# Leading halves of the first batch's keys and their 32x32 grams ahead of everything, with a layer norm spread through the order

## The reference

```
G = Kc.T @ Kc + 1e-4 * I ;  W = solve(G, Kc.T @ Vc)
U = eye[:, :8];  twice: U, _ = qr(W @ U)
S = 0.9 * S + U @ (U.T @ W)        # S is carried along the 8 chunks of a batch
out = 0.125 * (Qc @ S)
```

## Time and profile before

| | us |
|---|---|
| median of 3 runs (936.78 to 948.41) | 944.77 |
| the profiled execution | 943.76 |
| its span, first to last instruction | 941.7 |
| PE busy in it | 800.1 |
| DVE busy | 621.3 |
| ACT busy | 494.1 |
| POOL busy | 206.7 |

### The profile page before, as it was taken

How to read it: one execution, slowest core, us unless ns; L and a number is a source line. 1 busy time by engine, 2 the same in 40 slices (tenths; PEclk the granted TensorE clock), 3 DMA queues, 4 the chain that set the end, 5 groups by cost and what they waited for, 6 DMA issues and landing times.

```text
span 941.7 us, 36123 instructions
## 1 busy us (share of the span) xinstructions
PE 800.1 (85%) x15690; PEld 535.7 (57%) x15690; DVE 621.3 (66%) x1312; ACT 494.1 (52%) x1068; POOL 206.7 (22%) x265
## 2 busy tenths in 40 slices
PE   5999999999989999896798678783588789958896
PEld 2555555665555555564566457562466556746775
DVE  4880497299997999917566866888996201355664
ACT  2854444564544555544456455543357446636765
POOL 4550000101001100002101432542003101435554
PEclk9999999999988999998799989987599889979998
DMA  8742313753655655865442374311545543212210
GB/s 317 237 158 77 90 46 101 205 163 96 187 150 160 160 142 140 202 195 139 100 98 95 101 189 148 107 52 52 114 116 139 132 90 92 93 42 75 80 46 29
DMA packets 214348, 116.64 MB, mean 124 GB/s; under 512 B 149232, under 2 KB 200816, under 8 KB 213168
## 3 DMA queue, kind: packets, MB, share of 16 engines
q1 hardware_dynamic: 208720, 93.10, 36.5%
q0 software_dynamic: 5472, 21.24, 6.8%
HBM read 61.22 MB, written 53.08 MB: 121 GB/s over the span
## 4 chain that ended last, share of the span: by engine, by line
PE 71%; issue 9%; ACT 7%; DVE 6%; DMA 4%; POOL 2%; SPq 1%; POOLq 0%; DVEq 0%; ACTq 0%
PE psum L1188 23%; PE psum L1350 6%; PE psum L1210 5%; PE psum L1418 5%; PE psum L1408 5%; PE psum L1301 4%; PE psum L1388 3%; PE psum L1266 3%; PE psum L1253 2%; PE psum L1240 2%; PE psum L1288 2%; PE psum L1381 2%; PE psum L1324 2%; ACT ht L918 2%; PE psum L1374 1%
## 5 line engine op out<-in xcount | busy, mean ns | idle before, releaser
L1188 PE MATMUL psum<-wkv,xhat 128*128 128x512 f32 x512 | 245.0, 623 | 4.3 <-ACT xhat L783 4.3
L1049 DVE SCALAR_TENSOR_TENSOR outer<-sweep_mem,rd 128x992 f32<-128x992 f32 (+30 forms) x248 | 190.2, 767 | 8.7
L1055 DVE TENSOR_TENSOR sweep_mem<-sweep_mem,outer 128x992 f32<-128x992 f32 (+30 forms) x248 | 176.1, 710 | 8.5
L1188 PEld LDWEIGHTS psum<-wkv,xhat 128*128 128x128 f32 x512 | 95.4, 196 | 108.4 <-issue 102.9
L791 ACT COPY kv<-psum 128x512 f32<-128x512 f32 x128 | 75.0, 586 | 126.4 <-PE psum L1188 126.2
L918 ACT ACTIVATE ht<-psum,b1c,alpha 128x128 f32<-128x128 f32 x256 | 96.5, 461 | 42.4 <-PE psum L1408 42.4
L713 POOL TENSOR_TENSOR hsplit<-ht,hsplit 128x512 f16<-128x512 f32 x64 | 77.1, 1206 | 159.1 <-ACT hsplit L923 159.0
L1418 PE MATMUL psum<-s2t,hsplit 128*128 128x256 f16 x512 | 69.2, 293 | 5.4 <-POOL hsplit L713 2.7
L1408 PEld LDWEIGHTS psum<-y3t,s1t 128*128 128x128 f16 x1024 | 58.6, 99 | 13.0 <-issue 12.3
L1418 PEld LDWEIGHTS psum<-s2t,hsplit 128*128 128x128 f16 x512 | 53.1, 105 | 19.6 <-issue 6.6
L1408 PE MATMUL psum<-y3t,s1t 128*128 128x128 f16 x1024 | 64.0, 222 | 0.0
(11 more groups left out here) (128 smaller groups left out, 1237.4 us busy)
## 6 DMA issues: line engine op xcount, KB each, us to landing
gc_d<-gc SPq DMA_DIRECT2D x32, 512.0 KB, 3.1
schur_mem<-gc_d SPq DMA_DIRECT2D x32, 384.0 KB, 4.6
f_d<-fac SPq DMA_DIRECT2D x16, 512.0 KB, 3.7
fl<-f_d SPq DMA_DIRECT2D x32, 256.0 KB, 2.7
sv_d<-sv SPq DMA_DIRECT2D x16, 384.0 KB, 2.8
lead_d<-sweep_mem POOLq DMA_DIRECT2D x4, 1024.0 KB, 4.2
schur_mem<-lead_d SPq DMA_DIRECT2D x32, 128.0 KB, 4.3
r_d<-pt SPq DMA_DIRECT2D x16, 256.0 KB, 2.4
```

Source lines behind the costliest of these rows:

```text
L1049: V.scalar_tensor_tensor(out=tile, in0=a[:, t, t + 1:HALF].unsqueeze(2).broadcast_to([P, m, HALF]), scalar=rd[:, t:t + 1], in1=a[:, t, t + ...
L1055: V.tensor_tensor(rest, rest, tile, ALU.subtract).then_inc(swept, 1)
L1188: ins = mm(dst[:], xnt[:, c, t], wkv[:, n, t, BANK * half:BANK * (half + 1)], start=t == 0, stop=t == KT - 1)
```

## The change

1. The layer norm becomes steps LN of ORDER, with 17 groups of 1, 1 and 15 x 2 chunks. `advance_dve` puts one in while DVE's model time is within 4 us of PE's; once a sweep is staged and due, only if fewer than 4 chunks are ahead of the last T.
2. x now lies in pt, the residual in state, and the sweeps have a buffer of their own (work). POOL's wait for the residual stores goes. In its place ACT's evacuation of the first two SP steps waits for all 17 groups (pt is written there), and the first two state updates wait for the residual stores.
3. For the 8 chunks of batch 0 (EARLY = 8) the list begins with T, KL, LG of each chunk: KL projects the leading 32 columns of each head's keys, ACT copies them to keys, LG forms 16 grams of 32x32 from them (both operands 128 rows x 32 columns), ACT copies these to gl0 (in kv), SP stores them to lead_in_d. Then for each of these chunks KC (ACT places the kept leading keys in kv), KT (PE projects the trailing halves), VA, VB, G. The first sweep is staged after the eighth LG. KC of chunk 0 waits for the stores of all eight, as gl0 lies in kv.
4. gc_d no longer has the leading blocks and lies by partition (one piece of 3072 bytes for a chunk and partition). For chunks 8 to 31 ACT copies the leading block of G to gl separately and SP stores it to lead_in_d with two more DMAs.
5. The plan: it starts at 0 and not with fixed offsets; two small steps in a row cost 1.4 times; main stays ahead of tail and lead to its end (MIX_FROM 32); NB of batch 0, 1, 2, 3 is not put before 5, 6, 7, 8 sweeps are done in the plan. The new steps get weights (KL, KT 1.72 and LG .55 on PE; KC, KT, KL .65 and LG .35 on ACT, G 1.35 for 1.1).
6. fac, fl, nb and ht share the memory of keys.

The diff, cut to its core:

```diff
...
-GROUPS = (1, 3) + (4,) * 7
+GROUPS = (1, 1) + (2,) * 15
...
-PE_START, DVE_START = 10.0, 75.0
-MIX_FROM = 22
+EARLY = 8
+LN_WEIGHT = 1.75
+MIX_FROM = 32
+ALONE = 1.4
+TURNS_AFTER = (5, 6, 7, 8)
...
-    now = dict(pe=PE_START, act=PE_START, dve=DVE_START, pool=DVE_START)
+    now = dict(pe=0.0, act=0.0, dve=5.0, pool=5.0)
+    norms = list(range(len(GROUPS)))
+    latest = [""]
     def advance_dve():
+            while norms and now["dve"] <= now["pe"] + 4.0:
+                g = norms[0]
+                behind = FIRST[g] < sum(1 for c in range(NCH) if ("T", c) in where) + 4
+                if staged and staged[0][1] <= now["dve"] + 1.0 and not behind:
+                    break
+                norms.pop(0)
+                order.append(("LN", g))
+                now["dve"] = max(now["dve"], now["pe"] - 2.0) + LN_WEIGHT * GROUPS[g] + .6
+                for c in range(FIRST[g], FIRST[g] + GROUPS[g]):
+                    at["LN", c] = now["dve"]
...
     def follows(step, c):
-        return dict(KA=[("T", c)], KB=[("T", c)], VA=[("T", c)], VB=[("T", c)], G=[("VB", c)], SP=[("LC", c)], SX=[("SP", c)],
+        return dict(T=[("LN", c)], KL=[("T", c)], LG=[("KL", c)], KT=[("T", c)], KA=[("T", c)], KB=[("T", c)], VA=[("T", c)], VB=[("T", c)], G=[("VB", c)], SP=[("LC", c)], SX=[("SP", c)],
...
-            now["pe"] = can_start(step, c) + PE_WEIGHT[step]
+            now["pe"] = can_start(step, c) + PE_WEIGHT[step] * (ALONE if step in SMALL and latest[0] in SMALL else 1)
+            latest[0] = step
...
-        elif step == "G" and c % CPB == CPB - 1:
+        elif step == "LG" and c % CPB == CPB - 1:
+            open_at[0, c // CPB] = at["LG", c] + .5
+        elif step == "G" and c % CPB == CPB - 1 and c >= EARLY:
...
-    main = [("T", 0)]
+    main = [] if EARLY else [("T", 0)]
-        for step in ("KA", "KB", "VA", "VB", "T", "G"):
-            if step != "T" or c + 1 < NCH:
+        if c < EARLY and c % CPB == 0:
+            main += [("T", c), ("KL", c)]
+            for n in range(c + 1, c + CPB):
+                main += [("T", n), ("KL", n), ("LG", n - 1)]
+            main.append(("LG", c + CPB - 1))
+        for step in ("KC", "KT", "VA", "VB", "T", "G") if c < EARLY else ("KA", "KB", "VA", "VB", "T", "G"):
+            if step != "T" or EARLY <= c + 1 < NCH:
...
-    last = "T"
+        if turn in able and turn[0][0] == "NB" and sum(("swept", w, b) in at for w in range(2) for b in range(BATCH)
+                                                                         ) < TURNS_AFTER[TURNS[turn[0][1]] // CPB]:
+            able.remove(turn)
-        stream = large[0] if last in SMALL and large else able[0]
-        last = stream[0][0]
+        stream = large[0] if latest[0] in SMALL and large else able[0]
...
-    gc_d = scratch("gc_d", [NCH, PAIRS, P, P])
+    gc_d = scratch("gc_d", [P, NCH, PAIRS, 3 * HALF])
+    lead_in_d = scratch("lead_in_d", [NCH, HEADS, HALF, HALF])
...
-        sweep_mem = sb("sweep_mem", [P, 4 * 4 * DM])
-        xg = sweep_mem[:, 0:8 * DM].rearrange("p (a k d) -> p a k d", a=2, k=4)
-        lng = sweep_mem[:, 8 * DM:16 * DM].rearrange("p (a k d) -> p a k d", a=2, k=4)
-        work = sweep_mem[:].rearrange("p (a i n) -> p a i n", a=2, i=HALF)
+        work = sb("work", [P, 2, HALF, HD])
-        gc = sb("gc", [P, 2, PAIRS, P])
+        gc = sb("gc", [P, 2, PAIRS, 3 * HALF])
+        gl = sb("gl", [P, 2, PAIRS, HALF])
+        gl0 = kv[:, 0].rearrange("p (c n) -> p c n", n=P)
...
+        xg = pt[:].rearrange("p e c h n -> p (e c h n)").rearrange("p (a k d) -> p a k d", a=2, k=2)
...
-        fac = sb("fac", [P, 2, 2 * DM])
+        late = sb("late", [P, CPB * BANK])
+        keys = late[:].rearrange("p (c n) -> p c n", n=BANK)
+        fac = late[:, 0:4 * DM].rearrange("p (c n) -> p c n", n=2 * DM)
...
-        fl = sb("fl", [P, 3, 2 * DM])
-        nb = sb("nb", [P, 2, DM])
+        fl = late[:, 4 * DM:10 * DM].rearrange("p (a n) -> p a n", n=2 * DM)
+        nb = late[:, 10 * DM:12 * DM].rearrange("p (a n) -> p a n", n=DM)
+        lng = state[:].rearrange("p a (k d) -> p a k d", k=2)
-        ht = sb("ht", [P, FF])
+        ht = late[:, 12 * DM:16 * DM]
...
-                    sp.dma_start(gct[:, n, i], gc_d[c + i].rearrange("h r n -> r h n")[:, :, HALF:P]).then_inc(schur_loaded[n], 16)
+                    sp.dma_start(gct[:, n, i], gc_d[:, c + i]).then_inc(schur_loaded[n], 16)
...
-                src = gc_d[c:c + 2].rearrange("c (s u) r n -> u r c s n", u=2)
+                src = gc_d[:, c:c + 2].rearrange("r c (s u) n -> u r c s n", u=2)
-                        sp.dma_start(cu[rows(2 * a), u], src[u, rows(2 * a), :, :, HD:P]).then_inc(sides_loaded, 16)
+                        sp.dma_start(cu[rows(2 * a), u], src[u, rows(2 * a), :, :, HALF:]).then_inc(sides_loaded, 16)
             def load_factors(r):
...
-                    sp.dma_start(gc_d[c].rearrange("h r n -> r h n"), gc[:, c % 2]).then_inc(gc_stored[c % 2], 16)
+                    sp.dma_start(gc_d[:, c], gc[:, c % 2]).then_inc(gc_stored[c % 2], 16)
+                    if c >= EARLY:
+                        dst = lead_in_d[c].rearrange("(h a) r n -> a r h n", a=2)
+                        for a in range(2):
+                            sp.dma_start(dst[a], gl[rows(2 * a), c % 2]).then_inc(lead_in_stored[c % 2], 16)
+                elif step == "LG":
+                    sp.wait_ge(*is_drained("LG", c))
+                    sp.dma_start(lead_in_d[c].rearrange("(k q) r n -> (q r) k n", q=QUADS), pieces(gl0[:, c % CPB], HALF)
+                                 ).then_inc(lead_in_stored[c % 2], 16)
...
-            for g, size in enumerate(GROUPS):
+            def norm(g):
+                size = GROUPS[g]
...
-                else:
-                    for n in range(2):
-                        pool.wait_ge(res_stored[n], 16 * len(GROUPS[n::2]))
-                eye = sweep_mem[:, HALF * HD * (j % 2) + HALF:HALF * HD * (j % 2 + 1):HD + 1]
+                eye = work[:, j % 2].rearrange("p i n -> p (i n)")[:, HALF::HD + 1]
-                        pool.wait_ge(gc_stored[n], 16 * CPB // 2 * (b + 1))
-                    src = gc_d[CPB * b:CPB * (b + 1), :, :, 0:HALF].rearrange("c h (s r) n -> (c h s) r n", s=2)[:, 0:HALF]
+                        pool.wait_ge(lead_in_stored[n], 16 * CPB // 2 * (b + 1 + max(0, b + 1 - EARLY // CPB)))
+                    src = lead_in_d[CPB * b:CPB * (b + 1)].rearrange("c h r n -> (c h) r n")
...
-                if step == "SLOAD":
+                if step == "LN":
+                    norm(c)
+                elif step == "SLOAD":
...
+            def early_keys(c):
+                act.wait_ge(*is_filled("KL", c))
+                if c >= CPB:
+                    act.wait_ge(keys_placed, c - CPB + 1)
+                    act.wait_ge(*is_filled("LG", c - CPB))
+                nc.scalar.copy(keys[:, c % CPB], place("KL", c)).then_inc(drain("KL", c), 1)
+            def early_gram(c):
+                act.wait_ge(*is_filled("LG", c))
+                if c >= CPB:
+                    act.wait_ge(*is_filled("G", CPB - 1))
+                nc.scalar.copy(gl0[:, c % CPB], place("LG", c)[:, 0:P]).then_inc(drain("LG", c), 1)
+            def by_halves(c):
+                return kv[:, 0].rearrange("p (h u e) -> p h u e", u=2, e=HALF)
+            def place_keys(c):
+                if c % CPB == 0:
+                    for n in range(2):
+                        act.wait_ge(lead_in_stored[n], 16 * (c + CPB) // 2)
+                else:
+                    act.wait_ge(*is_filled("G", c - 1))
+                act.wait_ge(*is_drained("KL", c))
+                nc.scalar.copy(by_halves(c)[:, :, 0], pieces(keys[:, c % CPB], HALF)).then_inc(keys_placed, 1)
+            def late_keys(c):
+                act.wait_ge(*is_filled("KT", c))
+                nc.scalar.copy(by_halves(c)[:, :, 1], pieces(place("KT", c), HALF)).then_inc(drain("KT", c), 1)
             def projected(step, c, n, half):
...
             def gram(c):
-                nc.scalar.copy(gc[:, c % 2].rearrange("p h n -> p (h n)"), place("G", c)).then_inc(drain("G", c), 1)
+                src = pieces(place("G", c), P)
+                if c >= EARLY:
+                    wait(act, lead_in_stored[c % 2], 16 * EARLY // 2 + 32 * ((c - EARLY) // 2))
+                    nc.scalar.copy(gl[:, c % 2], src[:, :, 0:HALF])
+                nc.scalar.copy(gc[:, c % 2], src[:, :, HALF:]).then_inc(drain("G", c), 1)
             def signs(n):
...
             def leading_inverse(e):
+                if e < 2:
+                    act.wait_ge(res_ready, len(GROUPS))
...
-            for g, size in enumerate(GROUPS):
+            def norm(g):
+                size = GROUPS[g]
...
-                    dg = sweep_mem[:, HALF * HD * (j % 2):HALF * HD * (j % 2 + 1):HD + 1]
+                    dg = a.rearrange("p i n -> p (i n)")[:, ::HD + 1]
...
+                else:
+                    for n in range(2):
```

(48 more changed lines are left out.)

3 lines of the change are left out of this document (removed).

## The result

The changed kernel is slower: 972.4 us (median of 4 runs, 966.8 to 976.5) against 941.9 of the kernel before on the same chip (4 runs), a ratio of 1.029, interval 1.024 to 1.034. I had predicted 915.8. The profiled execution took 976.46 us, its span is 974.6: 32.9 more than before.

The account below looks back on a forecast made before the run. PE's work (800 of 941.7 us) and its 141.6 us without any set the time. 941.7 + 14.0 (front on PE) + 9 (ACT's stall) - 41 (idle filled) - 10 (clock) = 913.7, plus 2.1 outside: 915.8 us, range 880 to 956.

Parts of the forecast that it names:

- my 8.8: Front, PE: 7 new waits of 1.25 us, KL waiting for ACT to evacuate T, 8.8 us lost.
- 0.65 a chunk: Front, PE: LG's 32 records take 0.65 us a chunk, 5.2 us for 8 chunks; 1.97 kept for the range.
- rival 3: Front: holes between short bursts keep PE at half clock, 19 us more, 935 us in all; chance 0.07.
- 1 to 2 us per Schur load: DRAM loads: gc_d's new layout makes fewer, longer pieces, saving this four times on a sweep's way, off PE's.
- SP would be due 14 us after the sweep: After the first sweep (64 to 119): first SP due at 133, while layer norm groups last to 144.
- ACT's wait for the layer norm, 9 us: Behind sweep 1: ACT stands 11 us before evacuating the first SP, costing PE 9 us (0 to 26).
- Rival 4: Behind sweep 1: ACT's first SP evacuation held by the layer norm, PE stands 26 us, 974 us in all; chance 0.15.
- The table of sweeps: DVE's sweeps: first 64 to 119, third ending at 301, (1,1) at 435, (1,2) at about 500, (1,3) at about 690.
- before 560: Second half: a sign that the forecast is right, sweep (1,2) ending before 560 us.
- 86% for the 74%, 41 us gained: PE from 418 to 722: busy share rises as (1,2) ends earlier, 226.3 us of work in 263 (31 to 64 gained).
- rival 1: After main: the wait only moves, PE busy 80% for 74%, 21 us gained, 945.8 us in all; chance 0.22.
- 10 us by clock 0.96 for 0.87: PE from 418 to 722: fewer holes give a better clock, half of 21 us gained (0 to 21).

Follow-up runs that it names:

- e2: Changed kernel, with the plan told the layer norm's traced costs and the first two SP put behind the last layer norm group: 962.4 us.
- e11b: Changed kernel without early halves (EARLY = 0) and with the plan's price for two small steps in a row 1.2, not 1.4: 920.0 us.
- e3: Changed kernel with MIX_FROM 22 for 32, so tail and lead go ahead of main from chunk 22 on: 994.8 us.
- e1: Changed kernel without the early halves (EARLY = 0 for 8), all else of the change kept: 946.2 us.
- e6: Changed kernel with e2's layer norm weights, x in wqt not pt, and the wait for all LN moved from SP evacuation to Wq's preparation: 955.3 us.

## Why the prediction was wrong

Three steps failed: the place of SP at the front, the 41 us of idle PE that were to be gained in the second half, and the sign of the clock term. The 41 us were the costliest.

**Right: the front's small terms.** The waits for T were 9.2 us, of which the first, there before, is 2.3, so 6.9 for my 8.8; LG 0.46 for 0.65 a chunk, 3.7 for 5.2 in sum; the last LG ended at 43 for 45.6. An undisturbed group of two cost 4.9 us for 5. The clock stayed 1.00 there, so rival 3's rule didn't act. (The 7.06 us quoted for four steps is 7.08 in its row; nothing hangs on it. That the new layout of gc_d saves 1 to 2 us per Schur load was a guess: the median to landing went from 4.6 to 4.2.)

**Wrong at the front: "SP would be due 14 us after the sweep".** I took SP 0 to come when the sweep is really done. The list doesn't know when that is: DVE's model had 4.1 us for a group that takes 4.9 where nothing holds it, and the eleven groups of two ahead of the sweep took 62.7, 5.7 each (one took 8.1, as POOL was clearing and loading the sweep's buffer meanwhile). With the first two they are 13 groups and end at 76, not 64. PE was at SP 0 ten us before the sweep's end, and an engine that walks a fixed list stands there (22.6 us). I had priced ACT's wait for the layer norm, 9 us, and left out PE's wait for the sweep. Measured, ACT's cost 3.2 and the sweep's 22.6; the loss of the front was 32.7 of idle time for 17.8 (8.8 + 9). Rival 4 had the total right (974) with the wrong mechanism: with e2 it is the ruling one, 10.9 us, but then the time is 962. So its total was luck and is no support for it.

**The table of sweeps was near until 435.** Predicted and measured: (1,0) 191 and 204, (0,1) 246 and 259, (0,2) 326 and 327, (1,1) 380 and 385. It said itself that the fifth sweep would end at 435, where it had ended at 404; I didn't draw the consequence. Behind it (1,2) was to end at about 500; (0,3) took its turn and (1,2) ended at 607. By then the limit "before 560" of my own list of signs was broken.

**Wrong in the second half, the costliest step: "86% for the 74%, 41 us gained".** The 77.7 us of idle PE were read as missing work. The waits of PE from 418 to 722 in the kernel before show what they are made of:

```profile
PE psum L1278 <- DMA vv<-sv_d: 21.4, 1, 21.4
PE psum L1388 <- DVE state L1108: 8.9, 6, 3.0
PE psum L1396 <- DVE x L1129: 6.4, 2, 4.2
PE psum L1340 <- issue: 5.5, 4, 2.2
```

There is one hole of 21.4 us for want of a sweep. Added up from the timeline, about 52 of the 77.7 us are gaps of up to 3 us, between small steps that wait for an evacuation or just follow each other. The earlier sweep didn't touch these. The kernel after shows it: the hole is gone, the longest gap is 4.3 us, the gaps under 3 us add up to 54, and the same stretch has 69.1 us idle. Its waits, the longest in sum:

```profile
PE psum L1370 <- issue: 9.1, 5, 2.9
PE psum L1451 <- ACT y L957: 8.0, 4, 2.3
PE psum L1418 <- issue: 6.3, 3, 3.7
```

So 8.6 us for my 41 (77% busy, between the 74% and rival 1's 80%). Another order does touch the short gaps: in the same stretch e11b has 45 us of them and e3 34.

**Wrong in sign: "10 us by clock 0.96 for 0.87".** The clock was 0.82, and 0.75 and 0.78 in the first two thirds of the stretch (418 to 520 and 520 to 620, before 0.90 and 0.86). The first third, before and after:

```profile
418.00:520.00 102.00, 81.02 (x2911) 57.17 (x2908) 59.22 (x120) 53.29 (x127) 15.49 (x24) 0.90 0.45 110
```
```profile
418.00:520.00 102.00, 75.82 (x2664) 56.50 (x2666) 77.64 (x175) 44.39 (x96) 9.96 (x16) 0.75 0.53 132
```

Busy PE grew by 18.0 over the whole span, of which LG is 3.7. The list keeps main ahead of lead and tail to its end, so more of the small steps stand in this stretch (PE has 7443 records there for 6240, and 3318 for 4702 from 181.5 to 418). That these, with a gap each, lowered the clock is my reading: e3, which mixes them with main, had 0.94, but e1, with the same rule and no early halves, had 0.86. That the clock and not other work makes the remaining 14 us is worked out, not shown by a run of its own; for it speaks that the ten kernels with early halves have the same 15946 PE records and busy times from 794.1 (e3) to 818.2 us (e2).

**The sum again.** Predicted: 14 + 9 - 41 - 10 = -28. Measured: front +32.7 idle, 181 to 418 -10.1, 418 to 722 -8.6, behind that +1.2, busy PE +18.0: +33.2, the 32.9 of the spans but for rounding. The two sums are 61 us apart: 32 for the gain of 41 that was 8.6, 23 for busy PE (I had 5.2 for LG less 10 for the clock) and 15 for the front's idle time, less the 10 gained from 181 to 418, which I hadn't counted, and 1 more behind.

**What stays open.** Why one list gives 920 and another 946, with the same steps, isn't settled. The table has a regularity: with 14 to 16 turns begun by the last sweep's end the rest took 216 to 221 us in all nine kernels, with 11 or 12 it took 236 to 246, with 8 about 263, with 22 it took 178. So a kernel's time is the last sweep's end plus the turns it owes, and a list that ends its sweeps early by starving the turns gains nothing (e6, after). It describes the loss and says neither what causes it nor which rule makes a good list. The limits 5 to 8 on turns are not the cause: with 0 in their place the plan writes the same list for the changed kernel. A search over lists with the early halves wasn't made, so a list that makes them pay isn't excluded; seven fronts at the price 1.4 and two of them at 1.2 found none.

## What to carry to other kernels

Before counting on an earlier producer, ask which gaps of the busy engine it can fill: take the waits by their longest, not their sum, since here only the hole answered to an earlier sweep and the short gaps didn't. Where engines walk one list written ahead, a part that is moved forward is only as good as the plan's durations for what stands around it, and the first check is whether each consumer stands in the list behind the real end of its producer. And follow a change of order through the next sweeps to the end: here one sweep 30 us earlier made the fifth 35 us later.
